# Gate, up and down weights laid out transposed on the host, in a fused decoder layer on one Trainium2 core

## The reference

```python
W_gate, W_up: [1376, 512]    W_down: [512, 1376]
up   = einsum('td,fd->tf', xf, W_up)
gate = silu(einsum('td,fd->tf', xf, W_gate))
y    = einsum('tf,df->td', gate * up, W_down)
```

## Time and profile before

| | |
|---|---|
| three runs | 1030.24, 1030.61, 1031.05 us (median 1030.61) |
| the profiled execution | spans 1029.7 us from its first to its last instruction |
| PE busy | 1003.1 us, 97% of the span |
| DVE, ACT, POOL busy | 581.3, 428.1, 381.6 us |
| transfers | 39.98 MB, mean 39 GB/s |
| feed-forward block | from about 828.5 us to the end |

### The profile page before, as it was taken

The page is one execution under the profiler, slowest core; times in us unless marked ns, Lnnn a source line. Parts: engine busy times, 40 slices in busy tenths (PEclk is TensorE's granted clock), DMA queues, the critical chain, the costliest instruction groups (busy, mean ns, idle before and its releaser), DMA issues. The chain is left out here.

```text
span 1029.7 us, 16071 instructions
## 1 busy us (share of the span) xinstructions
PE 1003.1 (97%) x5260; PEld 822.9 (80%) x5260; DVE 581.3 (56%) x973; ACT 428.1 (42%) x1239; POOL 381.6 (37%) x375
## 2 busy tenths in 40 slices
PE   5999999989999999999999999999999999999998
PEld 3787777876888888888888888888887778888787
DVE  3765555636776666767666666766765852222101
ACT  2777666751533433533533434434334433332100
POOL 7422222253642642643634534626424222222100
PEclk8999999989999999999999999999999999999999
DMA  6000000211110210210210201201100022221001
GB/s 199 12 11 11 11 10 10 62 52 52 50 54 1 73 32 0 71 31 0 74 27 20 72 10 31 61 10 49 43 1 32 1 62 61 61 69 47 11 31 41
DMA packets 45699, 39.98 MB, mean 39 GB/s; under 512 B 3617, under 2 KB 34465, under 8 KB 45665
## 3 DMA queue, kind: packets, MB, share of 16 engines
q1 hardware_dynamic: 45280, 38.48, 12.7%
q0 software_dynamic: 384, 1.05, 0.3%
HBM read 37.43 MB, written 2.10 MB: 38 GB/s over the span
## 5 line engine op out<-in xcount | busy, mean ns | idle before, releaser
L624 PE MATMUL bank<-cross_wo_hl,cross_outT_hl 128*128 128x512 f32 x768 | 191.7, 398 | 1.0 <-POOL cross_wo_hl L618 0.6
L624 PE MATMUL bank<-hsT_hl,cross_wqkv_hl 128*128 128x512 f32 x768 | 188.2, 394 | 0.0
L624 PEld LDWEIGHTS bank<-cross_wo_hl,cross_outT_hl 128*128 128x128 f32 x768 | 143.1, 188 | 35.5 <-POOL cross_wo_hl L618 1.6
L624 PEld LDWEIGHTS bank<-hsT_hl,cross_wqkv_hl 128*128 128x128 f32 x768 | 141.9, 188 | 29.3
L938 ACT ACTIVATE cross_scores<-cross_scores,cross_negmax 128x128 f32<-128x128 f32 x256 | 99.8, 391 | 127.1 <-DVE cross_negmax L876 127.1
L798 POOL TENSOR_TENSOR cross_qT<-rotated,rotated_other_half 128x512 f32<-128x512 f32 x64 | 82.8, 1293 | 162.0 <-DVE rotated_other_half L840 162.0
L624 PE MATMUL bank<-hsT_hl,ff_gate_upT_hl 128*128 128x512 f32 (+1 forms) x528 | 126.3, 395 | 0.5 <-DVE ff_gate_upT_hl L1140 0.5
L624 PEld LDWEIGHTS bank<-hsT_hl,ff_gate_upT_hl 128*128 128x128 f32 (+1 forms) x528 | 96.3, 186 | 21.9 <-DVE ff_gate_upT_hl L1140 0.8
L948 ACT CAST cross_outT_hl<-bank 128x512 fp32r<-128x512 f32 x64 | 37.1, 579 | 143.4 <-PE bank L624 142.5
L838 DVE TENSOR_TENSOR rotated<-bank,cosT 128x512 f32<-128x512 f32 x80 | 55.2, 690 | 71.4 <-PE bank L624 71.2
L624 PE MATMUL bank<-ctxT_hl,cross_wqkv_hl 128*128 128x512 f32 x384 | 94.3, 394 | 1.1 <-PEq L74 1.1
(11 more groups left out here) (121 smaller groups left out, 1565.7 us busy)
## 6 DMA issues: line engine op xcount, KB each, us to landing
staged_rows<-in_wq SPq DMA_DIRECT2D x32, 256.0 KB, 2.8
staged_rows<-in_wo SPq DMA_DIRECT2D x32, 256.0 KB, 2.7
staged_rows<-in_wg SPq DMA_DIRECT2D x10, 256.0 KB, 2.6
staged_rows<-in_wu SPq DMA_DIRECT2D x10, 256.0 KB, 2.8
staged_rows<-in_wd SPq DMA_DIRECT2D x10, 256.0 KB, 3.0
ctx_tok<-in_ctx SPq DMA_DIRECT2D x8, 256.0 KB, 2.6
staged_rows<-in_wk SPq DMA_DIRECT2D x8, 256.0 KB, 3.1
staged_rows<-in_wv SPq DMA_DIRECT2D x8, 256.0 KB, 3.1
```

What stands on the lines that cost most here:

```text
L624: i = nc.tensor.matmul(out, stationary[:, a], moving[:, b], start=(first and k == 0), stop=(last and k == 2))
```

## The change

The host now lays out the three weights as the tiles want them (`laid_out`): gate and up padded with zero rows to 1408 features and stored as 11 tiles [128, 512] that already are what the four transposes made; down stored transposed, 11 tiles [128, 512]. A load brings one such tile, 2 KB to a partition, always for 128 partitions. PE transposes no weights any more, and the semaphores of the transposes go. ACT's high parts wait for the load itself and read the landed rows in SBUF; DVE's low parts subtract from the landed rows too, not from a bank. A slot is loaded again when its low part has been made (before: when its transposes had been made). The order of all other work on each engine is the same.

```diff
 def load_ff_rows(sp, m, sem, io, i):
-    n = width_of(i)
-    at = i * P if isinstance(i, int) else sp.snap(i * P)
+    at = i if isinstance(i, int) else sp.snap(i)
     for k, name in enumerate(("wg", "wu")):
         if not (isinstance(i, int) and i == 0):
-            sp.wait_ge(sem["w_transposed"], 2 * i + k - 1)
-            if k == 1:
-                sp.wait_ge(sem["wd_transposed"], i)
-        sp.dma_start(m["gate_up_rows"][0:n, k, :], io[name][bass.ds(at, n), :]).then_inc(sem[f"{name}_loaded"], 16)
-    sp.dma_start(m["down_rows"][:, :, 0:n], io["wd"].rearrange("(t p) f -> p t f", p=P)[:, :, bass.ds(at, n)]).then_inc(sem["wd_loaded"], 16)
+            sp.wait_ge(sem["w_low"], 2 * i + k - 1)
+        sp.dma_start(m["gate_up_rows"][:, k, :], io[name][bass.ds(at, 1)].rearrange("i p n -> p (i n)")).then_inc(sem[f"{name}_loaded"], 16)
+    if not (isinstance(i, int) and i == 0):
+        sp.wait_ge(sem["wd_low"], i)
+    sp.dma_start(m["down_rows"], io["wd"][bass.ds(at, 1)].rearrange("i p n -> p (i n)")).then_inc(sem["wd_loaded"], 16)
...
             def w_low(i, k):
-                nc.vector.tensor_tensor(wT[:, k, 1, :, 0:n], TW[k][:].rearrange("p (t f) -> p t f", t=KT)[:, :, 0:n],
+                nc.vector.tensor_tensor(wT[:, k, 1, :, 0:n], raw[:, k, :].rearrange("p (t f) -> p t f", t=KT)[:, :, 0:n],
...
-                nc.vector.tensor_tensor(wdT[0:n, 1, bass.ds(i, 1), :], TD[0:n, :].unsqueeze(1), wdT[0:n, 0, bass.ds(i, 1), :].bitcast(F32),
+                nc.vector.tensor_tensor(wdT[0:n, 1, bass.ds(i, 1), :], rawd[0:n, :].unsqueeze(1), wdT[0:n, 0, bass.ds(i, 1), :].bitcast(F32),
...
             def w_high(i, k, first=False):
-                act.wait_ge(sem["w_transposed"], 2 * i + k + 1)
+                act.wait_ge(sem["wu_loaded" if k else "wg_loaded"], 16 * i + 16)
...
-                nc.scalar.copy(wT[:, k, 0, :, 0:n], TW[k][:].rearrange("p (t f) -> p t f", t=KT)[:, :, 0:n]).then_inc(sem["w_high"], 1)
+                nc.scalar.copy(wT[:, k, 0, :, 0:n], raw[:, k, :].rearrange("p (t f) -> p t f", t=KT)[:, :, 0:n]).then_inc(sem["w_high"], 1)
...
-                act.wait_ge(sem["wd_transposed"], i + 1)
-                nc.scalar.copy(wdT[0:n, 0, bass.ds(i, 1), :], TD[0:n, :].unsqueeze(1)).then_inc(sem["wd_high"], 1)
+                act.wait_ge(sem["wd_loaded"], 16 * i + 16)
+                nc.scalar.copy(wdT[0:n, 0, bass.ds(i, 1), :], rawd[0:n, :].unsqueeze(1)).then_inc(sem["wd_high"], 1)
...
         def _(pe):
-            def w_transposes(i, k, first=False):
...
             def body(i, first=False):
-                w_transposes(i, 1, first)
-                pe.wait_ge(sem["wd_loaded"], 16 * i + 16)
-                if not first:
-                    pe.wait_ge(sem["wd_low"], i)
-                for t in range(KT):
-                    e = nc.tensor.transpose(TD[0:n, t * P:(t + 1) * P], rawd[:, t, 0:n], ident[:])
-                e.then_inc(sem["wd_transposed"], 1)
...
-                    w_transposes(i + 1, 0)
...
-            w_transposes(0, 0, first=True)
...
+def laid_out(given):
+    given["pos"] = given["pos"].T
+    rows = FT * P - FF
+    for name in ("wg", "wu"):
+        given[name] = np.pad(given[name], ((0, rows), (0, 0))).reshape(FT, P, KT, P).transpose(0, 3, 2, 1).reshape(FT, P, DM)
+    given["wd"] = np.pad(given["wd"].T, ((0, rows), (0, 0))).reshape(FT, P, DM)
+    return {name: np.ascontiguousarray(a) for name, a in given.items()}
```

## The result

The changed kernel takes **1016.12 us** (median of four runs, 1015.36 to 1016.59) where the kernel before took 1030.42 beside it (1029.58 to 1031.05): ratio 0.986, interval 0.9846 to 0.9874, 14.3 us less.

What follows compares the result with a forecast made beforehand. TensorE (PE), busy 97% of the span, was taken as the bound: -13.4 us for the transposes and +1.2 for a clock fall at the block's start give -12.2, so 1030.61 becomes 1018.4 us; range 1016.8 to 1020.4.

Steps and rivals of the forecast that it cites:

- The bound: Whole kernel: PE is busy 97% of the span; in the feed-forward block each transpose stands on the path with its full step.
- The transposes' term: Feed-forward tiles 1 to 10: 120 weight transposes go, 112 ns apiece, 13.4 us less (13.0 as the low end).
- The split: Middle tiles: up's low part, read from SBUF, ends at T + 3.7 at worst, wanted at T + 5.47; cost nothing.
- The loads: Feed-forward weight slots, refilled 1 to 2.5 us later: up has 5 us to spare; cost nothing.
- The start: Feed-forward block's start: first matmul 0.34 us earlier, but a 2.74 us hole on PE and DVE's low parts beside POOL.
- the case without a fall: Block's start with the clock staying: 0.34 us won, or 0.3 lost if DVE and POOL exclude each other.
- the price put on it: Block's start: two low parts hold off POOL's power, so 0.3 us lost instead of 0.34 won.
- The clock: Behind the 2.74 us hole at the block's start PE's clock falls to half speed: 1.2 us later; chance 0.57.
- a longer one: Rival: the clock falls at the block's start and returns only at 838, 1.7 us more, 1020.1 us; chance 0.11.
- the clock stays: Rival: no fall behind the hole at the block's start; 1016.9 us, or 1017.5 with DVE and POOL excluding; chance 0.25.
- split in PE's place: Rival: in each of ten tiles PE waits for up's low part; 1040 us at 4 us later; chance 0.04 with in-between cases.
- growth of the matmul step: Rival: PE's queue needed the pauses, so the step grows; half the gain would leave 1024 us; chance 0.03.

Runs made afterwards that it cites:

- the delayed split: The changed kernel with six more copies of 512 columns on ACT ahead of each high part of up, from tile 1 on: 1034.57 us.

## Why the prediction was right or wrong

**The bound: right.** PE's row was the path, and transposes on it were worth their step.

**The transposes' term: right in kind, 0.5 us too small.** 13.4 was worked out, 13.92 measured. The size that was off is the step of a matmul. The prediction took 0.2278 from the 312 matmuls behind the tiles, most of which are y's. In the changed kernel the two kinds stand side by side:

```profile
848.70 101.65 PE L624 MATMUL bank<-hsT_hl,ff_gate_upT_hl 128*128 128x512 f32 x447
950.19 60.17 PE L624 MATMUL bank<-ff_downT_hl,ff_hT_hl 128*128 128x512 f32 x264
```

Gate and up take (950.19 - 848.70) / 447 = 0.2270 each, y takes 60.19 / 264 = 0.2280 (to the end of the chain's piece at 1010.38). With 0.2270 the stretch holds 100.8 us of matmuls and 13.7 of transposes. The last 0.2 us I can't place.

**The split: right.** Its end was put at T + 3.7 at worst and came at T + 3.5, with DVE held off by POOL; nothing waits for it, and the delayed split shows that the cover is of the size worked out. What lies past the cover is paid in each tile, as forecast; one delay was tried, at 1.25 us a tile.

**The loads: right.** No engine waits for a load in this block after the change.

**The start: right but for the clock.** The first low part and with it the DVE chain came 0.3 to 0.4 us earlier, as in the case without a fall. Beside a low part, which now reads SBUF twice, POOL waited: its addition beside the first one took 0.54 us (0.19 in the earlier trace rows), its power beside the next 0.88 instead of 0.55. The Trainium skill, SBUF — State Buffer, section Who interferes with whom, has it that a VectorE instruction with two SBUF inputs and a GpSimd instruction that reads SBUF exclude each other; these rows and the middle tile agree with it. But the price put on it, 0.6 us of the start, was wrong: the power was over at 831.85, while DVE was still at the low part of down, and the rows 9 began at 831.97 as DVE came free. It was held off by one low part only, not by both.

**The clock: the step that failed.** "A hole of 2.74 is longer than the one that cost the clock, so I expect it to fall here" took one fall behind 1.84 us, among other work, for a limit. The hole came out at 2.66 us, and the clock fell in 4 of 32 executions, two of them inferred, and in none of the changed kernel's own twelve. Behind 3.68 and 4.17 us it fell in the one profile of each, and by their times in the other three executions of each; behind the 1.05 us at this place no profile shows a fall. So 0.57 for the fall (and 0.11 for a longer one) should have been near 0.15, and the 1.2 us belonged to a rival. The price of a fall was if anything low: 1.5 us against the case without one, where the executions that had it lie 2.5 to 4.2 us higher.

The trace of before already spoke against a limit. The fall that the earlier trace rows shows from its end, near 27 us, began in the slice from 20 to 21, behind a hole of 1.15 us, shorter than 1.84:

```profile
19.66 1.36 PE L498 MATMUL bank<-self_k_by_head_hl,self_qT_high_above_low 128*128 128x512 f32 x4 [1.15 <-POOL self_k_by_head_hl L181]
...
20.00:21.00 1.00, 1.00 (x4) 0.34 (x2) 0.60 (x1) 0.00 (x0) 0.92 (x2) 0.73 0.00 0
```

And in the profile of the changed kernel the clock stays at 1.00 at the same place, behind 1.16 us and then behind 1.88:

```profile
23.23 0.63 PE L433 MATMUL bank<-ident,xn 128*128 128x128 f32 x4 [1.88 <-POOL xn L158]
...
24.00:26.00 2.00, 2.00 (x11) 1.17 (x9) 1.93 (x5) 1.97 (x6) 1.76 (x4) 1.00 0.00 0
```

So the length of one hole does not decide alone whether the clock falls; what else does stays open.

Without this step the prediction's own sum reads -13.4 - 0.34, 1016.9; with the right matmul step -13.7 - 0.34, 1016.6, the slowest of the measured runs. The rival "the clock stays" named the mechanism and came within 0.8 us of the result, but the range ended at its better half, with no room for the error of the step.

**The other rivals** did not come: no split in PE's place, no growth of the matmul step.

## What to carry to other kernels

Price a transpose, or any instruction on a row that never rests, by the step it adds to the chain, and take the neighbours' step from the same kind of work: here a transpose added 0.112 to 0.118 us where its duration reads 0.27. A hole that opens on PE when work is removed is worth a line of its own, but one observed fall of the clock gives no limit: look at several holes, and give the fall a chance rather than a sum. Work of DVE that reads SBUF where it read PSUM may meet POOL; ask whether there is cover where it does.

## What the hardware showed

That the same hole, 2.66 us at the same place, is followed by a fall of TensorE's clock in some executions and not in others (4 of 32 with the two inferred), while each of the three profiles with a hole of 3.68 us or more between matmul products (3.68, 4.17 and the 4.66 of the delayed split) shows one, had not been expected. What the executions differ in is not settled here. Nor had it been expected that fp32r matmuls take 0.2270 us each in one stage and 0.2280 in the next, at a granted clock of 1.00 in both; why is open.
